# Adjacency aggregation with a top-2 expert layer in fp32: run ends filled chunk by chunk from SBUF, gate stages moved forward in a block, final sums on POOL

## The reference, cut to what matters

```python
def reference(x, adj, item_feat, W_item, b_item, W_user, b_user, gate_w, gate_b, W1, b1, W2, b2):
    u = _layernorm(x, axis=-1)                          # x: 10000 x 128, adj: 10000 x 10000
    h = item_feat @ W_item.T + b_item
    x = x + relu(adj @ h + (u @ W_user.T + b_user))
    xf = _layernorm(x, axis=-1)
    probs = softmax(xf @ gate_w + gate_b)               # 8 experts
    top2_vals, top2_idx = top_k(probs, 2)
    # each row: sum over its two experts of prob * (gelu(xf @ W1[e] + b1[e]) @ W2[e] + b2[e]), HID = 256
    return x + that_sum
```

## Time and profile before

| what | value |
|---|---|
| median of 3 runs | 1591.74 us (1587.52 to 1594.39) |
| the profiled execution, own time | 1596.78 us |
| its span, first to last instruction | 1594.9 us |
| mean granted TensorE clock | 0.985 of full |
| `adj` loads | 520 of 750 KB |
| DMA in all | 502.29 MB, mean 315 GB/s |

### The profile page before, as it was taken

The page is one execution under the profiler, slowest core; times in us unless marked ns, Lnnn a source line. Parts: engine busy times, 40 slices in busy tenths (PEclk is TensorE's granted clock), DMA queues, the critical chain, the costliest instruction groups (busy, mean ns, idle before and its releaser), DMA issues.

```text
span 1594.9 us, 20673 instructions
## 1 busy us (share of the span) xinstructions
PE 1495.0 (94%) x6682; PEld 1163.9 (73%) x6682; DVE 1280.3 (80%) x1677; ACT 1103.5 (69%) x1178; POOL 806.5 (51%) x596
## 2 busy tenths in 40 slices
PE   8999999999999999999999599999999989998887
PEld 6777777777776767767777488888888877776555
DVE  5768778788877887887788488888888978787898
ACT  5657757667666676666675578787878768786665
POOL 0114534643644446335443258785877766686420
PEclk9999999999999999999999899999999999999999
DMA  9889998999999999999998899999999998886675
GB/s 336 297 290 330 338 341 321 350 345 336 357 334 332 337 341 339 345 326 346 336 337 296 302 321 329 329 332 336 325 329 321 328 327 296 284 286 208 201 244 191
DMA packets 144649, 502.29 MB, mean 315 GB/s; under 512 B 35696, under 2 KB 41792, under 8 KB 144286
## 3 DMA queue, kind: packets, MB, share of 16 engines
q1 hardware_dynamic: 127518, 479.25, 85.9%
q0 software_dynamic: 17024, 21.73, 3.9%
HBM read 468.77 MB, written 36.31 MB: 317 GB/s over the span
## 4 chain that ended last, share of the span: by engine, by line
PE 35%; DVE 18%; DMA 18%; issue 9%; POOL 9%; ACT 8%; SPq 2%; ACTq 0%; DVEq 0%; POOLq 0%
DMA s_raw<-adj 16%; DVE s_a_lo L952 10%; PE p_agg L502 9%; PE p_agg L497 8%; PE p_agg L498 8%; ACT s_a_hi L743 5%; POOL rr L1353 3%; POOL zs L1344 2%; DVE s_h_hi L1178 2%; POOL s_rs L1315 1%; ACT s_rows L788 1%; PE p_hid L479 1%; PE p_hid L590 1%; PE p_hid L592 1%; PE p_hid L591 1%
## 5 line engine op out<-in xcount | busy, mean ns | idle before, releaser
L952 DVE TENSOR_TENSOR s_a_lo<-s_raw,s_a_hi 128x1500 fp32r<-128x1500 f32 x520 | 887.2, 1718 | 193.7 <-ACT s_a_hi L743 157.3
L743 ACT ACTIVATE s_a_hi<-s_raw 128x1500 fp32r<-128x1500 f32 x520 | 751.8, 1454 | 283.3 <-DMA s_raw<-adj 272.2
L497 PE MATMUL p_agg<-s_a_hi,s_h_hi 128*128 128x500 f32 x1560 | 633.4, 406 | 31.8 <-ACT s_a_hi L743 31.5
L498 PE MATMUL p_agg<-s_a_hi,s_h_lo 128*128 128x500 f32 x1560 | 610.7, 391 | 0.0
L502 PE MATMUL p_agg<-s_a_lo,s_h_hi 128*128 128x500 f32 x1560 | 456.9, 401 | 33.6 <-DVE s_a_lo L952 24.0
L1344 POOL DMA_INDIRECT zs<-s_rows,s_idx x136 | 243.3, 1789 | 287.2 <-DVE s_idx L1080 237.5
L502 PEld LDWEIGHTS p_agg<-s_a_lo,s_h_hi 128*128 128x128 f32 x1560 | 283.6, 190 | 143.1 <-DVE s_a_lo L952 91.8
L497 PEld LDWEIGHTS p_agg<-s_a_hi,s_h_hi 128*128 128x128 f32 x1560 | 297.2, 191 | 108.7 <-ACT s_a_hi L743 53.1
L1353 POOL DMA_INDIRECT rr<-s_ysb,s_dests x192 | 275.8, 1436 | 143.3 <-DVE s_ysb L1163 91.5
L498 PEld LDWEIGHTS p_agg<-s_a_hi,s_h_lo 128*128 128x128 f32 x1560 | 297.3, 191 | 55.3 <-issue 2.5
L1335 POOL TENSOR_TENSOR s_gt<-s_ebase,s_gt 125x32 f32<-125x32 f32 x20 | 125.7, 6283 | 52.1 <-DVE s_gt L1006 51.9
(11 more groups left out here) (215 smaller groups left out, 1406.1 us busy)
## 6 DMA issues: line engine op xcount, KB each, us to landing
s_raw<-adj SPq DMA_DIRECT2D x520, 750.0 KB
s_wraw<-w SPq DMA_DIRECT2D x72, 256.0 KB
s_zt<-zs SPq DMA_DIRECT2D x48, 264.0 KB
s_raw<-rr SPq DMA_DIRECT2D x34, 256.0 KB, 4.2
s_xtok<-x_tok SPq DMA_DIRECT2D x20, 256.0 KB
s_xt<-x_t SPq DMA_DIRECT2D x20, 250.0 KB, 6.6
out_s<-s_x1s SPq DMA_DIRECT2D x17, 256.0 KB
s_raw<-out_s SPq DMA_DIRECT2D x17, 256.0 KB, 3.7
```

The lines of the kernel that those rows point to most:

```text
L497: mm(o, h_hi[:, k * D:(k + 1) * D], hi, start=(k == 0), stop=False)
L498: mm(o, h_lo[:, k * D:(k + 1) * D], hi, start=False, stop=False)
L743: fn(a_hi[:, n % HIS, :], raw[:, n % RAW, :], ACT.Copy).then_inc(hi_made, 1)
L952: tt(a_lo[:, n % LOS, :], raw[:, n % RAW, :], a_hi[:, n % HIS, :].bitcast(F32), ALU.subtract)\
```

## The change

Five things are changed. (1) `fill_ends` becomes `fill_end(g, e)`: one run end per chunk, at n = 339 to 346 and 469 to 476, and from an SBUF buffer, `fill`, instead of from DRAM. (2) `fill` lies in `early` (set up once the buffer's first use is over, on POOL at n = 52), no longer in `ysb`; `big`, the table's scratch, moves to `gt`. (3) The stages of the gate stand at chunks 0 to 15 of a block instead of 1 to 20. (4) The first tile of each group stands at n = 350 and 480 instead of 348 and 478. (5) The final sums are made by POOL after all sends, with `rstd(BLOCKS)` before them and `power(BLOCKS - 1)` after the third of them; they are loaded two steps later (COMB_AT) and stored two steps after their load instead of three.

```diff
-X1_AT, X1T_AT, BN2_AT, BN1_AT, X1S_AT, LG_AT, LN2_AT = 1, 1, 4, 5, 4, 9, 10
-TAILHI_AT, TAILLO_AT, SOFT_AT, TOP1_AT, TOP2_AT, LN1_AT = 9, 10, 15, 16, 17, 13
-PREFIX_AT, LN1T_AT, SLOT_AT, LN1C_AT = 18, 16, 20, 19
-TABLE_AT = (20, 21, 22)
+X1_AT, X1T_AT, BN2_AT, BN1_AT, X1S_AT, LG_AT, LN2_AT = 1, 0, 3, 3, 3, 7, 8
+TAILHI_AT, TAILLO_AT, SOFT_AT, TOP1_AT, TOP2_AT, LN1_AT = 9, 10, 11, 12, 13, 10
+PREFIX_AT, LN1T_AT, SLOT_AT, LN1C_AT = 13, 12, 15, 15
+TABLE_AT = (15, 16, 17)
...
-FILL_AT = [(hi + 1) * CH + 5 for lo, hi in GROUPS]
-FIRST_W1 = [(hi + 1) * CH + 10 for lo, hi in GROUPS]
+FILL_AT = [(hi + 1) * CH + 1 for lo, hi in GROUPS]
+FIRST_W1 = [at + E + 3 for at in FILL_AT]
...
-ZT_LOAD = [0, 0] + [max(W1_AT[k - 2] + 3, FILL_AT[k >= NTG[0]] + 1) for k in range(2, NT)]
-COMB_AT = [p + p // CB for p in range(S)]
+ZT_LOAD = [0, 0] + [max(W1_AT[k - 2] + 3, FILL_AT[k >= NTG[0]] + E) for k in range(2, NT)]
+COMB_AT = [2 + p + p // CB for p in range(S)]
...
-        early = sb("early", [P, 3 * D])
+        early = sb("early", [P, SUBS * W])
...
-        fill = ysb[:, :, :].rearrange("p a n -> p (a n)")[:, 0:SUBS * W].rearrange("p (s w) -> p s w", w=W)
+        fill = early[:, :].rearrange("p (s w) -> p s w", w=W)
...
-        big = early[0:1, 0:NTG[0] * E]
+        big = gt[0:1, :, :].rearrange("p a n -> p (a n)")[:, 0:NTG[0] * E]
...
-            def fill_ends(g):
-                sp.wait_ge(scattered, 2 * 16 * SUBS * GROUPS[g][1])
-                sp.wait_ge(tab_made, 2 * (g + 1))
-                sp.wait_ge(spare_filled, 16 * 2)
-                for e in range(E):
-                    r = sp.value_load(fillat[0:1, g, e:e + 1], min_val=0, max_val=SPARE0[g] - T)
-                    sp.dma_start(zs[bass.ds(r, T), :].rearrange("(p s) w -> p (s w)", s=SUBS),
-                                 zs[SPARE0[g]:SPARE0[g] + T, :].rearrange("(p s) w -> p (s w)", s=SUBS))\
-                        .then_inc(filled, 16)
+            def fill_end(g, e):
+                if e == 0:
+                    sp.wait_ge(scattered, 2 * 16 * SUBS * GROUPS[g][1])
+                    sp.wait_ge(tab_made, 2 * (g + 1))
+                r = sp.value_load(fillat[0:1, g, e:e + 1], min_val=0, max_val=SPARE0[g] - T)
+                sp.dma_start(zs[bass.ds(r, T), :].rearrange("(p s) w -> p (s w)", s=SUBS),
+                             fill.rearrange("p s w -> p (s w)")).then_inc(filled, 16)
...
-                    if n == FILL_AT[g_]:
-                        fill_ends(g_)
-                if n == FILL_AT[0] + 1:
+                    if 0 <= n - FILL_AT[g_] < E:
+                        fill_end(g_, n - FILL_AT[g_])
+                if n == FILL_AT[0] + E:
                     load_w(0)
                     load_w(1)
...
-                    if COMB_AT[p] == j - 3:
+                    if COMB_AT[p] == j - 2:
                         comb_store(p)
...
-                for p in range(S):
-                    if COMB_AT[p] == d - 2:
-                        comb_add(p)
...
+            def comb_add(p):
+                pool.wait_ge(comb_loaded[p % CB], 16 * 3 * (p // CB + 1))
+                gp.tensor_tensor(comb(p, 1), comb(p, 1), comb(p, 2), ALU.add).then_inc(comb_mid, 1)
+                pool.wait_ge(comb_mid, p + 1)
+                gp.tensor_tensor(comb(p, 0), comb(p, 0), comb(p, 1), ALU.add).then_inc(comb_made, 1)
...
                     if YOUT_AT[k] == n:
                         send(k)
-                        if k == NT - 3:
-                            rstd(BLOCKS)
-                        if k == NT - 2:
-                            power(BLOCKS - 1)
+                if n == 2 * CH:
+                    pool.wait_ge(h_prod, CH + 1)
+                    pool.wait_ge(gsum_done, 1)
+                    pool.wait_ge(bb_split, 1)
+                    gp.memset(fill, 0.0).then_inc(fill_set, 1)
+                    pool.wait_ge(fill_set, 1)
+                    gp.tensor_scalar(fill[:, :, D + 1], dest0[:, :], float(DUMP + 2 * T), None, ALU.add)\
+                        .then_inc(fill_set, 1)
+            rstd(BLOCKS)
+            for p in range(S):
+                if p == CB:
+                    power(BLOCKS - 1)
+                comb_add(p)
```

More of the change, by code:

```diff
@@ L204, in build @@
         b2_hi, b2_lo, b2_split = sem("b2_hi"), sem("b2_lo"), sem("b2_split")
-        gsum_done, gatec_made, base_set, spare_set, spare_filled = (
-            sem("gsum_done"), sem("gatec_made"), sem("base_set"), sem("spare_set"), sem("spare_filled"))
+        gsum_done, gatec_made, base_set, spare_set, spare_filled, fill_set = (
+            sem("gsum_done"), sem("gatec_made"), sem("base_set"), sem("spare_set"), sem("spare_filled"),
+            sem("fill_set"))
         tail_hi, tail_split = sem("tail_hi"), sem("tail_split")
@@ L411, in _ @@
                 if n == 22:
-                    sp.wait_ge(spare_set, 4)
+                    sp.wait_ge(spare_set, 3)
                     ends = rr[0:DUMP, :].rearrange("(b r) d -> b (r d)", r=T)
@@ L417, in _ @@
                 if n == 3 * CH + 3:
-                    sp.wait_ge(spare_set, 4)
+                    sp.wait_ge(fill_set, 2)
                     for g_ in range(2):
@@ L784, in ln2_norm @@
                 if p == 0:
-                    act.wait_ge(sets, 5)
+                    act.wait_ge(sets, 4)
                 r = rows[0] if p < S else rows[(p - S) % 2]
@@ L1147, in ext @@
                 if k == 0:
-                    dve.wait_ge(spare_set, 4)
+                    dve.wait_ge(spare_set, 3)
                 tt(dests[:, k % XR, :], zt[:, k % 2, :, D + 1], pads[:, k % 2, :], ALU.min).then_inc(ext_made, 1)
@@ L1158, in y_out @@
                 dve.wait_ge(ext_made, 2 * (k + 1))
-                if k == 0:
-                    dve.wait_ge(spare_filled, 16 * 2)
                 if k >= 2:
@@ L1183, in dense_out @@
                 tt(x, dy(q)[:, 0:UB], x, ALU.add).then_inc(out_made, 1)
[L1185 to L1189, removed]
             def items(n):
@@ L1363, in _ @@
             gp.memset(rows[1][:, :, :], 0.0).then_inc(sets, 1)
-            gp.memset(ysb[:, :, :], 0.0).then_inc(sets, 1)
-            pool.wait_ge(sets, 5)
+            pool.wait_ge(sets, 4)
             pool.wait_ge(late_loaded, 16 * NL)
-            gp.tensor_scalar(fill[:, :, D + 1], dest0[:, :], float(DUMP + 2 * T), None, ALU.add).then_inc(spare_set, 1)
             for i in range(2):
@@ L1372, in _ @@
             rstd(0)
-            pool.wait_ge(spare_set, 4)
+            pool.wait_ge(spare_set, 3)
             for n in range(LAST):
```

## The result

The kernel after takes 1642.48 us (median of 4 runs, 1636.68 to 1649.38) against 1593.07 for the kernel before (4 runs, 1587.52 to 1599.12): ratio 1.0305, 95% interval 1.0269 to 1.0342. It is 49 us slower. Forecast were 1583 us and a range of 1566 to 1597. Both were wrong.

The account below looks back on a forecast made before the run. The `adj` stream was taken to pace the streaming stretch, PE and DMA the tile stretch, DVE mostly the dense steps. Terms -5.6 + 0 - 6.9 + 3.4 = -9.1 us from 1591.74 gave 1582.6, said as 1583; range 1566 to 1597.

Parts of the forecast that it names:

- The stages moved: Gate stages at earlier chunks: x1's turn +1.7 us and softmax +1.7 us, sum +3.4 us (0 to 29).
- In the streaming stretch PE has slack: Turning x1 after PE's chunk 0 costs nothing in streaming blocks; only waits in blocks 18 and 19 were charged, +1.7 us.
- distances from `rstd` to the logits stay at four chunks: Gate stages: the unchanged distance between POOL's `rstd` and the logits was given no cost.
- Softmax behind `power`: Softmax four chunks after the logits instead of six: DVE waits 4.8 us, a lead covers 3.1, +1.7 us once.
- the slower rival: Softmax waits for POOL's `power` in each of six tile blocks, 29 us: total +18, 1610 us; chance 0.12.
- the prediction's own warnings: Wrong if dense stretch stays at 97 us, POOL additions exceed 1.6 us undisturbed, or streaming blocks change their 2.45 us a chunk.
- The first fill: Hole at 866 to 905 us: -13.5 for the hole, +6.4 for writes, +1.5 at n = 347; -5.6 us (-13.5 to 0).
- The second fill: In the full stretch, remaining write time less a chunk's lead about equals the 3.9 us idle now: 0 (-3.9 to +4).
- The final sums: Dense tail with sums on POOL: -14.2 gain, +4.3 exclusion, +3 SP's stand; -6.9 us.
- the open question: Whether POOL's additions also hold up DVE: +4.3 us (0 to 36) if exclusion works both ways, 0 by the trace's rows alone.
- 3.67 us a step: Dense steps without the additions: 23 steps at the loop's 3.67 us take 84.4 us instead of 97.3.
- SP's stand before the weights: Dense tail: SP waits at `comb_store` for POOL's sum with weight loads behind it, +3 us (0 to 5.8).

Follow-up runs that it names:

- s3: The kernel before with the new places of the gate stages alone: 1637.7 us, ratio 1.0284.
- s1: The kernel after with the gate stages back at their old chunks and the fills four chunks later: 1591.34 us, ratio 0.9999.
- s6: The kernel before with X1T_AT alone at 0, so x1 is turned before PE's chunk 1: 1620.17 us, ratio 1.0171.
- s13: s5 with the logits and all that hangs on them two chunks later, fills included: 1596.22 us, ratio 1.0020 against before.
- s5: The kernel after with X1T_AT alone back at 1, so PE turns x1 after chunk 1: 1605.68 us, ratio 1.0071 against before.
- s7: The fills alone: the kernel after with old gate stages, fills four chunks later, and the final sums back on DVE: 1579.4 us, ratio 0.9917.
- s2: The kernel after with the final sums back on DVE, loaded and stored in the old steps: 1637.29 us, ratio 1.0265 against before.
- s4: The kernel before with the final sums on POOL alone: 1601.19 us, ratio 1.0049.
- s11: The kernel before with one small POOL memset added at the end of POOL's program: 1600.75 us, ratio 1.0047.

## Why the prediction was wrong

**The stages moved: +3.4 us forecast, +45 to +49 measured (s3; after less s1).** This is the step that failed, in two places. "In the streaming stretch PE has slack" was the sentence by which x1's turn cost nothing in 12 of 19 blocks. PE was idle 5% of that stretch, but slack as a share doesn't help an instruction that another engine feeds: PE waits behind DVE's chunk 1, DVE is then held by its two `a_lo` buffers, and the loads hang on DVE. I had looked at the wait (1.9 us in the earlier trace rows) and not at who is queued behind it, and I had found the stretch bound by the stream, where any stop of line 952's instruction that lasts longer than its lead is time. X1T_AT alone: 27 us (s6), 37 in after. The second was "distances from `rstd` to the logits stay at four chunks". The distance stayed, but the room in it did not: `rstd` now falls into the chunks in which DVE catches up. POOL's 0.20 us under three such subtractions took 4.87 us in the earlier trace rows, which I used for the tail alone. In after this is 34.4 us of waiting before the logits against 16.2; s13 takes such a wait, 30.1 us, away from s5 and wins 9.5 us (8 by the ratios).

**Softmax behind `power`: +1.7 us, and the slower rival.** The rival's mechanism did not come. In after only block 18 has a wait of DVE for POOL before the softmax, of 2.3 us. It named the right side and the wrong stage. Two of the prediction's own warnings came true: the streaming blocks changed their 2.45 us a chunk, and the dense stretch did not fall below 97 us.

**The first fill: -5.6 us, measured -13 (s7, both fills).** The mechanism was right, only a term was mis-sized: of the writes' own 6.4 us, charged in full, over half fitted beside the stream. Blocks 13 to 17 are 13.5 us shorter in s7, which equals the upper bound of the gain, but by luck: it is 18.8 us in block 13 less 5.3 in the four behind it, and neither number stood in the forecast. Beside the new stages the fills bring only 3 us (s3 less s2), which the two intervals do not tell from nothing. Block 13 is at 86.0 us in s3 already: the moved slots let the scatter end sooner, and SP's wait for it, 4.7 us in before, is gone (its loads of `adj` end at 908.94, the fills begin at 910.02). Of the 8.2 us that s2 wins there over s3, blocks 14 to 17 give back 6.5. **The second fill: 0**; block 18 wins 5.3 us in s7, and blocks 14 and 15 lose 9.7. Which of the edits costs there, the later first tile or the tile loads behind the last fill, was not separated.

**The final sums: -6.9 us, measured +8 (s4), +6 (after less s2).** Four terms failed. First, the addition takes 1.26 us at its shortest, not 1.05. The 1.11 us estimated from the GPSIMD Engine Reference of the Trainium skill, its section on elementwise work, were nearer and still low. Second, exclusion holds in both directions, which had been the open question, and the earlier trace rows, with tiny reads on POOL alone, had been no evidence against it. I had charged 4.3 us; DVE's two lines alone are 12 us longer in after (15 in s4, 56.6 for 41.4), because it strikes both of them in a step, and even small instructions. DVE and POOL of after in order of time, within the dense steps:

```profile
1575.86 1.43 DVE L1175 TENSOR_TENSOR s_h_hi<-s_g,s_h_hi 128x1000 fp32r<-128x1000 f32 x1
1577.21 1.77 DVE L1134 TENSOR_TENSOR s_wt<-s_wraw,s_wt 128x512 fp32r<-128x512 f32 x1
1578.90 1.27 DVE L1031 TENSOR_TENSOR s_gt<-s_gt,s_col 125x32 f32<-125x32 f32 x1
```

```profile
1576.31 2.12 POOL L1329 TENSOR_TENSOR s_raw<-s_raw 128x512 f32<-128x512 f32 x1
1578.39 1.74 POOL L1327 TENSOR_TENSOR s_raw<-s_raw 128x512 f32<-128x512 f32 x1
```

Each waits for the other in turn: POOL's addition ends 1.14 us after line 1175 does, line 1134 ends 0.55 us after that addition, and line 1031 only with POOL's next one, each about its own time behind the other. The page SBUF — State Buffer of the Trainium skill, in Who interferes with whom, says this: a DVE instruction with two SBUF inputs and a GpSimd one that reads SBUF shut each other out for whole instructions. The trace agrees on both sides now: 2.12 for 1.26, and 1.77 for 0.68. Third, 3.67 us a step was no floor where DVE also does the gate of block 19: the steps d = 10 to 13 took 20.2 us in before and 24.0 in s4, where the forecast has 14.7 (4 x 3.67). That is 9.3 of the 14.8 us by which s4's dense steps lie above 84.4. SP's stand before the weights, +3 in the forecast, shows once in them: in step 10 of s4 ACT waits 2.86 us for a load and DVE 1.88 for ACT. And fourth, the program's end: POOL's DRAIN, 5 us, and SP at `comb_store`, behind POOL's last sum, 2.9 us (`out_d` at 1633.83, made at 1630.93). No term stood for either; both were put at nothing without a reason. The dense steps did not get shorter: 97.3 us before, 99.2 in s4, 100.4 in after, for a forecast of 91.7 (84.4 + 4.3 + 3).

**The sum.** By parts alone, -13 + 45 + 8 = +40; measured +49. The 9 us between them are mostly the fills' gain of 13, which is only 3 beside the new stages. The median of before is 1593.07 in this comparison and 1591.74 in the forecast's; no more than these 1.3 us of the miss lie there.

## What to carry to other kernels

Before an instruction is moved forward on an engine with idle time, find its input's maker and the work between the two: if the mover then waits ahead of work whose buffers hold the bound engine or the stream, the wait is paid each time round the loop (27 to 37 us here, for a PE with 5% of idle time). A fixed distance from a POOL step to its reader is worth only as much as DVE leaves it: look at what DVE runs back to back in between. And work that reads SBUF, moved from DVE to POOL beside two-input DVE work, cost more here than it gave, at the program's end above all.

## What the runs showed of the hardware

POOL's DRAIN at the end of the program took at least 7.3 us after its last instruction, a 0.10 us memset in s11, so a late POOL instruction moves the end by 5 us where it is otherwise the last engine but SP. A 128x512 addition on POOL takes 1.26 us at its shortest, against 0.69 on DVE, and up to 2.2 beside it. The exclusion also strikes instructions of 0.19 us: line 1031 took 1.27. And the DMA engines moved 369 GB/s over 39 us with writes from SBUF beside the loads of `adj`, where the loads and their usual company had run at 338.
